# A vision block with routed experts on one core: blocks without a GpSimd drain, fill rows written in the block before, expert stage skewed by two more pairs

## The chip, the cores and the metric

One Trainium2 chip; the program runs on one of its cores, in one launch. The metric is device microseconds of that core for one execution, the median over the runs. The engines are TensorE (PE, with PEld for its weight loads), VectorE (DVE), ScalarE (ACT), GpSimd (POOL) and SyncE (SP), which here only issues transfers. Each engine runs its own instruction stream in order and meets the others through semaphores.

## The reference

The input is 64 images; each is cut into 196 patches of 768 numbers, so there are S = 64 x 196 = 12544 tokens of width D = 256.

```python
h = einsum('bnk,ek->bne', patches, W) + b                  # tokens
h = h + ssm(layernorm(h))                                  # x = A_bar*x + Bu, y = C x + D u
x = layernorm(h)
y1 = ln(x + mha(x)) * g1 + be1                             # 4 heads, attention over the 64 images
# routing: 8 experts, each takes its first S // 8 tokens
gates = softmax(y1 @ wg); idx = argmax(gates)
loc = rank of the token among those of its expert; keep = loc < S // 8
y = (y1 @ w1[idx] + b1[idx]) @ w2[idx] + b2[idx]           # no nonlinearity between
y2 = ln(y1 + where(keep, gate * y, 0)) * g2 + be2
out = h + y2
```

## The kernel before

In the profile a block's end stands at the line at which its scope closes: L155 (weights split, constants built), L304 (after block A), L721 (after block B), L1183 (the program's end).

**Block A** computes the tokens and the state space layer for 49 groups of 256 tokens, and beside it folds each expert's two matrices into one 256 x 256 matrix (`w12`, and `b12` for the biases), since there is no nonlinearity between them.

**Block B** computes attention, the first layer norm, the gate and the token's place in its expert's bin, for 49 groups, with up to six groups in flight. GpSimd writes every group's rows into `bins` in DRAM with two indirect transfers (`send`, L908). A row has 515 numbers: y1, the residual h1, the gate, the token's order S and the token's number (`OFF_I`). At its end GpSimd waits until all have landed (L917 and after), and VectorE makes running counts for the ranks (L1043 to L1051).

**Block C** is the expert stage. It begins with a stretch of set-up: TensorE sums the counts (L1424) and the ranks (L1427 to L1429); VectorE turns the counts into the first free row of each bin (`fi`, L1326) and into two tables that say for each of 106 tiles of 128 rows where its rows are (`tab_r`) and whose weights it takes (`tab_e`, L1345), and then into the threshold beyond which a token is dropped (`tile_thr`, L1360). SP and ACT fill 128 rows behind the last token of each bin (9 transfers, L1231, L1235, L1289), so that a tile may read past a bin's end. TensorE runs 20 matmuls with no use for their result (L1434) as soon as the tables are there.

Then come 53 pairs of tiles. Each engine runs a loop of steps; in step k it does some stages for pair k, others for pair k-1 or k-2 (`k.back(n)`). The stages, with what they wait for:

- SP `load` (L1245): both tiles of a pair into one of 8 row buffers `row`, when the pair 8 earlier has been sent and its transfers have landed (`sent`).
- PE `turn_y` (L1442): 4 transposes of y1 into `c_ps_t`. ACT `y_out` (L1255): their copy into `yt`. PE `experts` (L1454, L1457): 10 matmuls whose weights are picked by registers, loaded from `tab_e` (L1448).
- DVE `keep` (L1366, L1369): gate, or zero for a dropped token. ACT `weighted` (L1263): product times gate.
- DVE `residual` (L1375), `stats` (L1380), `mean` (L1387); ACT `dev` (L1270); DVE `scale` (L1393), `shift` (L1398); ACT `norm` (L1277); DVE `gain` (L1404), `finish` (L1411): layer norm, and the sum with h1 into one of 8 buffers `res`.
- POOL `send` (L1304): two indirect transfers into `out`, with the token numbers read from the row buffer.

The steps of before, from the code of ACT, DVE and PE:

```python
# ACT
for m, stage in ((k, y_out), (k.back(1), weighted), (k.back(2), norm), (k.back(1), dev)):
# DVE
for m, stage in ((k.back(2), shift), (k.back(1), residual), (k.back(1), stats), (k.back(1), mean),
                 (k.back(2), gain), (k, keep), (k.back(2), finish), (k.back(1), scale)):
# PE
for m, stage in ((k.back(1), experts), (k, turn_y)):
```

So PE's order is experts(k-1), turn_y(k), experts(k), and experts(k) needs ACT's copy of what turn_y(k) has just written. An engine's order within a step is fixed; nothing schedules it again. Between steps 8 and 48 the loop is a real one with eight steps in its body.

## Time and profile before

| | |
|---|---|
| median of 3 runs | 1417.65 us (1417.57 to 1417.94) |
| the profiled execution | 1416.46 us |
| its span, first to last instruction | 1414.6 us |
| busy in the span | PE 1261.9, PEld 1142.2, DVE 1030.3, ACT 735.8, POOL 711.5 us |
| mean granted TensorE clock | 0.967 of full |
| block C | from 1152.88 us to the end, 261.7 us |

The profiled execution took 1.19 us less than the median, and 1.86 us of it lie outside the span. Busy times are sums over the whole program, in which four stages with different limits follow each other; the stage that the change touches most is the last, block C, and its set-up.

### The profile page before, as it was taken

The page shows a single profiled execution, that of the slowest core. Times are in us where ns is not written, and L with a number is a line of the kernel's source. Part 1 is how long each engine was busy: PE and PEld are TensorE (multiplying, and loading weights), DVE is VectorE, ACT ScalarE, POOL GpSimd, SP SyncE. Part 2 cuts the span into 40 slices and gives each one's busy share as a digit, 9 for nine tenths or more (in the row PEclk, how much of TensorE's full clock was granted, in tenths as well). Part 3 has the DMA queues.
Part 4 walks back from the last instruction along what each step waited for, and adds up shares of the span by engine and source line. Part 5 has one row for each costly group of instructions (what it writes and reads, how often), then busy time and mean ns, then how long its engine had stood idle before and what let it go on. Part 6 is the DMA issues. An engine that isn't in the chain of part 4 may idle for free. (4 is left out here: it accounts for less than half of the span.)

```text
span 1414.6 us, 37211 instructions
## 1 busy us (share of the span) xinstructions
PE 1261.9 (89%) x11790; PEld 1142.2 (81%) x11791; DVE 1030.3 (73%) x2787; ACT 735.8 (52%) x1515; POOL 711.5 (50%) x913
## 2 busy tenths in 40 slices
PE   2999999999999997699999999999999638788783
PEld 2999999999999997599999999999999525455452
DVE  4578878877887777467777777777777556777774
ACT  3465565555555555354555555455545205665663
POOL 1566656656665663135445544544554323455454
PEclk9999999999999999799999999999999759999997
DMA  7435453545455432122323232322222136666661
GB/s 237 151 113 157 145 188 112 175 138 176 141 157 175 128 104 95 40 72 96 102 92 104 93 100 89 104 97 97 97 97 97 68 109 184 194 182 184 184 185 35
DMA packets 97044, 180.07 MB, mean 127 GB/s; under 512 B 12319, under 2 KB 62497, under 8 KB 95970
## 3 DMA queue, kind: packets, MB, share of 16 engines
q1 hardware_dynamic: 82244, 138.66, 32.6%
q0 software_dynamic: 13312, 39.75, 7.7%
q10 hardware_dynamic: 1440, 1.07, 0.2%
q8 instruction: 23, 0.38, 0.1%
q14 instruction: 25, 0.20, 0.1%
HBM read 112.69 MB, written 67.80 MB: 128 GB/s over the span
## 5 line engine op out<-in xcount | busy, mean ns | idle before, releaser
L476 POOL TENSOR_TENSOR xl<-xf,xh 128x512 fp32r<-128x512 f32 x141 | 178.9, 1298 | 204.6 <-ACT xh L402 204.6
L1304 POOL DMA_INDIRECT out<-res,row x106 | 123.0, 1160 | 116.7 <-DVE res L1411 99.1
L297 PE MATMUL ps_h<-wh,xh 128*128 128x256 f32 x588 | 166.4, 283 | 4.9 <-DVE xl L613 4.9
L297 PE MATMUL ps_h<-wh,xl 128*128 128x256 f32 x588 | 166.4, 283 | 0.0
L297 PE MATMUL ps_h<-wl,xh 128*128 128x256 f32 x588 | 166.1, 283 | 0.0
L1454 PE MATMUL c_ps_y<-w,yt 128*128 x424 | 119.6, 405 | 45.5 <-ACT yt L1255 45.5
L843 ACT ACTIVATE zn<-z,nm_z,rs_z 128x256 f32<-128x256 f32 x98 | 53.6, 594 | 200.6 <-DVE nm_z L972 200.6
L908 POOL DMA_INDIRECT bins<-rows,slot_i x98 | 101.1, 1031 | 60.2 <-POOL slot_i L902 45.2
L1454 PEld LDWEIGHTS c_ps_y<-w,yt 128*128 128x128 f32 x424 | 72.0, 189 | 69.9 <-issue 57.8
L297 PEld LDWEIGHTS ps_h<-wh,xh 128*128 128x128 f32 x588 | 111.9, 190 | 5.6 <-DVE xl L613 5.6
L297 PE MATMUL b<-x2h,wh 128*128 128x256 f32 x392 | 114.3, 292 | 0.0
L297 PEld LDWEIGHTS ps_h<-wl,xh 128*128 128x128 f32 x588 | 111.8, 190 | 0.0
L297 PEld LDWEIGHTS ps_h<-wh,xl 128*128 128x128 f32 x588 | 111.6, 190 | 0.0
L297 PE MATMUL b<-x2l,wh 128*128 128x256 f32 x392 | 110.3, 281 | 0.0
L297 PE MATMUL b<-x2h,wl 128*128 128x256 f32 x392 | 110.3, 281 | 0.0
L926 DVE TENSOR_TENSOR x2l<-ps_o,x2h 128x512 fp32r<-128x512 f32 x49 | 33.9, 691 | 95.2 <-ACT x2h L848 95.2
L882 POOL TENSOR_TENSOR x2b<-x,rows_c 128x512 f32<-128x512 f32 x49 | 63.3, 1292 | 61.2 <-DVE z L958 58.4
L902 POOL CAST slot_i<-small 128x2 int32<-128x2 f32 x49 | 9.0, 184 | 159.5 <-DVE small L1020 159.5
L531 DVE TENSOR_TENSOR_SCAN xs<-decay,xs,bu 128x256 f32<-128x256 f32 x96 | 66.9, 738 | 29.6 <-ACT bu L414 29.4
L438 ACT ACTIVATE nrm_x<-mv_xa,c_eps 128x2 f32<-128x2 f32 x49 | 14.5, 296 | 141.0 <-DVE mv_xa L591 141.0
L492 POOL TENSOR_TENSOR h1b<-h1o,rows_c 128x512 f32<-128x512 f32 x49 | 79.4, 1622 | 10.1 <-DVE h1o L578 10.1
L539 DVE TENSOR_TENSOR sl<-xs,sh 128x512 fp32r<-128x512 f32 x49 | 79.9, 1632 | 0.0
(254 smaller groups left out, 4388.9 us busy)
## 6 DMA issues: line engine op xcount, KB each, us to landing
xf<-xt SPq DMA_DIRECT2D x49, 768.0 KB, 5.3
row<-bins SPq DMA_DIRECT2D x106, 257.5 KB, 3.0
h_dram<-h1b SPq DMA_DIRECT2D x49, 256.0 KB, 5.2
x_dram<-x2o SPq DMA_DIRECT2D x49, 256.0 KB, 5.3
x<-x_dram SPq DMA_DIRECT2D x98, 128.0 KB, 2.8
rows<-h_dram SPq DMA_DIRECT2D x98, 128.0 KB, 2.8
w1s<-w1t SPq DMA_DIRECT2D x8, 1024.0 KB, 6.8
w2s<-w SPq DMA_DIRECT2D x8, 516.0 KB, 5.3
```

The costliest lines, as they stand in the source:

```text
L297: last = nc.tensor.matmul(out_ps, a, b, start=(i == 0), stop=(i == len(terms) - 1))
L438: nc.scalar.activation(nrm_x[:, 0, :], mv_x[:, :, 1], ACT.Sqrt, bias=c_eps[:]).then_inc(x_sd, 1)
L476: last = nc.gpsimd.tensor_tensor(xl[:, p, part], xf[:, p, part], xh[:, p, part].bitcast(F32), ALU.subtract)
L492: nc.gpsimd.tensor_tensor(h1b[:, p], h1o[:, p], r_be2.unsqueeze(1).to_broadcast([P, 2, D]), ALU.add).then_inc(h1b_done, 1)
L531: v.tensor_tensor_scan(xs[:, p, t, :], decay[:, t, bass.ds(m.n() * G % N, G)], bu[:, p, t, :], 0.0 if first else xs[:, 1 - p, t, G - 1:G], ...
L539: v.tensor_tensor(sl[:, p, :], xs[:, p].rearrange("p t g -> p (t g)"), sh[:, p, :].bitcast(F32), ALU.subtract).then_inc(s_lo, 1)
L843: A(zn[:, s, :], z[:, s, :], ACT.Identity, bias=nm_z[:, s:s + 1], scale=rs_z[:, s:s + 1]).then_inc(Q["zn"], 1)
L882: g.tensor_tensor(x2b[:, p], x2[:, p], r_bo.unsqueeze(1).to_broadcast([P, 2, D]), ALU.add).then_inc(Q["x2b"], 1)
L908: g.indirect_dma_start(bins, bass.IndirectOffsetOnAxis(ap=slot_i[:, p, s:s + 1], axis=0), rows[:, p, s, :], None).then_inc(scattered[p], 16)
L926: v.tensor_tensor(xl[:], b_2, xh[:].bitcast(F32), ALU.subtract).then_inc(Q["x2lo"], 1)
L1304: g.indirect_dma_start(out, bass.IndirectOffsetOnAxis(ap=row[:, b, i, OFF_I:OFF_I + 1].bitcast(I32), axis=0), res[:, b, i, :], None, bound ...
L1454: mm(ps_y[p][:, i, :], yt[:, p, i, t * P:(t + 1) * P], w12[:, bass.ds(e, 1), t * D:(t + 1) * D].rearrange("p a d -> p (a d)"), start=(t == ...
```

## The change

It does five things.

2. The fill rows are written at the end of block B, by SP and ACT, and the counts that they need are summed there (PE into `b_4`, DVE into `cnt`, `past`, `fi`, ahead of the running counts for the ranks). GpSimd no longer waits at the end of block B for its transfers; SP does, at the start of block C.
3. In block C, PE runs 40 matmuls without a use in place of 20, and doesn't wait for the tables before them. PE's step becomes turn_y(k), experts(k-1). ACT and DVE take most stages one or two pairs later, in a new order.
4. A row buffer is free for the next load when DVE's `finish` has read it (`res_s`) and GpSimd has copied its two columns of token numbers into `idx` (new stage `index`, L1315 of the changed kernel), not when the transfers out of it have landed.
5. In block A, DVE waits for the experts' second bias (`fb_in`) before its loop, not within the first turn of it.

```diff
-            blk = ...(nc.Block())
+            blk = ...(nc.Block(no_gpsimd_drain=True))      # in all four blocks
@@ block A, DVE
-                        if isinstance(k.t, int):
-                            dve.wait_ge(fb_in, 16)
...
+                dve.wait_ge(fb_in, 16)                      # after the first two x_lo
@@ block B, SP, after its loop
                 run(sp, step, 0, NG + 2, 6, 46)
+                sp.dma_start(bins[BINS:BINS + P, :], fill[:]).then_inc(filled, 16)
+                sp.wait_ge(fi_ready, 1)
+                for e in range(NE // 2):
+                    r = sp.value_load(fi[0:1, e:e + 1], min_val=0, max_val=BINS)
+                    sp.dma_start(bins[bass.ds(r, P), :], fill[:]).then_inc(filled, 16)
@@ block B, ACT, after its loop
+                act.wait_ge(fi_ready, 1)
+                for e in range(NE // 2, NE):
+                    r = act.value_load(fi[0:1, e:e + 1], min_val=0, max_val=BINS)
+                    act.dma_start(bins[bass.ds(r, P), :], fill[:]).then_inc(filled, 16)
@@ block B, GpSimd, after its loop
-                for i in range(2):
-                    pool.wait_ge(scattered[i], 32 * ((NG + 1 - i) // 2))
@@ block B, DVE, after its loop
+                dve.wait_ge(cnt_ps, 1)
+                v.tensor_copy(cnt[:], b_4[:, 0:NE]).then_inc(cnt_out, 1)
+                dve.wait_ge(cnt_out, 1)
+                v.tensor_tensor(past[:], cnt[:], ebase[:], ALU.add).then_inc(past_done, 1)
+                dve.wait_ge(past_done, 1)
+                v.tensor_copy(fi[:], past[:]).then_inc(fi_ready, 1)
@@ block B, PE, after its loop
+                pe.wait_ge(Q["acc"], 2 * NG)
+                pe.wait_ge(Q["k_out"], 2 * NG)
+                mm(b_4[:, 0:NE], ones_b[:], oh_acc[:], start=True, stop=True).then_inc(cnt_ps, 1)
@@ block C, SP
-                (fill rows)
+                for i in range(2):
+                    sp.wait_ge(scattered[i], 32 * ((NG + 1 - i) // 2))
                 sp.wait_ge(filled, 16 * (NE + 1))
                 sp.wait_ge(tab_ready, 1)
...
-                            wait(sp, sent[b], k.turn(DEPTH) * 32)
+                            wait(sp, res_s, k.n() + 1 - DEPTH)
+                            wait(sp, idx_s, k.n() + 1 - DEPTH)
@@ block C, ACT
-                    for m, stage in ((k, y_out), (k.back(1), weighted), (k.back(2), norm), (k.back(1), dev)):
+                    for m, stage in ((k.back(4), dev), (k, y_out), (k.back(4), norm), (k.back(2), weighted)):
@@ block C, GpSimd
+                def index(k):
+                    b = k.slot(DEPTH)
+                    wait(pool, loaded[b], (k.turn(DEPTH) + 1) * 32)
+                    wait(pool, sent[b], k.turn(DEPTH) * 32)
+                    apart(pool, passed["pool"])
+                    g.tensor_copy(idx[:, b, :], row[:, b, :, OFF_I].bitcast(I32)).then_inc(idx_s, 1)
...
+                def step(k):
+                    for m, stage in ((k.back(-1), index), (k, send)):
@@ block C, DVE
-                dve.wait_ge(cnt_ps, 1)                      # counts, past, fi: now in block B
...
-                    for m, stage in ((k.back(2), shift), (k.back(1), residual), (k.back(1), stats), (k.back(1), mean),
-                                     (k.back(2), gain), (k, keep), (k.back(2), finish), (k.back(1), scale)):
+                    for m, stage in ((k.back(3), residual), (k.back(2), keep), (k.back(3), stats), (k.back(4), gain),
+                                     (k.back(3), mean), (k.back(4), finish), (k.back(3), scale), (k.back(3), shift)):
@@ block C, PE
-                pe.wait_ge(tab_ready, 1)
-                for _ in range(20):
+                for _ in range(40):
                     mm(ps_c[:], wh[:, 0:P], wh[:, 0:2 * D], start=True, stop=True)
...
-                    for m, stage in ((k.back(1), experts), (k, turn_y)):
+                    for m, stage in ((k, turn_y), (k.back(1), experts)):
```

The loops of ACT, DVE and PE run to `PAIRS + 4`, `PAIRS + 4` and `PAIRS + 1`. Buffers `rows`, `slot_i`, `cnt` and `fi` move to a scope that outlives block B.

On TensorE, around the end of the first pair's expert matmuls in block C (`c_ps_y0` is the product of an even pair, `c_ps_t0` and `c_ps_t1` hold the transposes of even and odd pairs). Before:

```order
L1454 MATMUL c_ps_y0<-w12,yt 128x256
L1457 ISA
L1457 MATMUL c_ps_y0<-b12s,two_rows 128x256
L1442 MATMUL c_ps_t1<-ident,row 128x128 x4
L1448 TENSOR_LOAD tab_e
```

And now, at the same place:

```order
L1471 MATMUL c_ps_y0<-w12,yt 128x256
L1474 ISA
L1474 MATMUL c_ps_y0<-b12s,two_rows 128x256
L1459 MATMUL c_ps_t0<-ident,row 128x128 x4
L1465 TENSOR_LOAD tab_e
```

Behind the product of pair 0 stood the transposes of pair 1; now those of pair 2 stand there, and pair 1's were done ahead of it.

On VectorE, one step of block C before:

```order
L1398 SCALAR_TENSOR_TENSOR c_nm<-c_mv,c_rs 128x2
L1375 TENSOR_TENSOR c_z<-c_py,row 128x512
L1380 BN_STATS c_st<-c_z 128x6 x2
L1387 BN_AGGR c_mv<-c_st 128x2 x2
L1404 TENSOR_TENSOR c_zg<-c_zn,rows_c 128x512
L1366 TENSOR_TENSOR c_below<-row,tile_thr 128x2
L1369 TENSOR_TENSOR gk<-c_below,row 128x2
L1411 TENSOR_TENSOR res<-c_zg,row 128x512
L1393 RECIPROCAL c_rs<-c_ve 128x2
```

And now:

```order
L1394 TENSOR_TENSOR c_z<-c_py,row 128x512
L1385 TENSOR_TENSOR c_below<-row,tile_thr 128x2
L1388 TENSOR_TENSOR gk<-c_below,row 128x2
L1399 BN_STATS c_st<-c_z 128x6 x2
L1423 TENSOR_TENSOR c_zg<-c_zn,rows_c 128x512
L1406 BN_AGGR c_mv<-c_st 128x2 x2
L1430 TENSOR_TENSOR res<-c_zg,row 128x512
L1412 RECIPROCAL c_rs<-c_ve 128x2
L1417 SCALAR_TENSOR_TENSOR c_nm<-c_mv,c_rs 128x2
```

The nine operations are the same. Between an operation and the one that needs it there now stands another, except for the two pairs of very small ones.

On SyncE, where block B ends and block C begins (L721 is the block's end). Before:

```order
L786 DMA rows<-h_dram 64x2x256 x10
L721 UNCONDITIONAL_BRANCH
L1228 UNCONDITIONAL_BRANCH
L1231 DMA bins<-fill 128x515
L1234 TENSOR_LOAD fi
```

And now:

```order
L789 DMA rows<-h_dram 64x2x256 x10
L801 DMA bins<-fill 128x515
L804 TENSOR_LOAD fi
L804 ISA x2
L805 ISA
```

The fill transfers stand ahead of the block's end now.

## Rows read from the trace of the kernel before

**Rows 1.** The page's chain that ended last, by engine, line and share of the span.

```profile
PE c_ps_y L1454 8%; PE c_ps_y L1457 2%; PE c_ps_t L1442 2%; ACT yt L1255 2%; POOL out L1304 0%; DMA bins<-fill 0%; DMA row<-bins 0%; ACTq L1288 0%; ACT c_py L1263 0%; DVE c_st L1380 0%; ACTq L1289 0%; DVE c_z L1375 0%; SPq L1242 0%; DVE res L1411 0%; DVE c_zg L1404 0%
```

**Rows 2.** Windows: us, busy PE, PEld, DVE, ACT, POOL, clock, DMA share, GB/s.

```profile
1144.00:1164.00 20.00, 5.55 (x15) 3.50 (x16) 9.99 (x24) 0.00 (x0) 0.22 (x1) 0.50 0.33 119
1168.00:1390.00 222.00, 177.08 (x732) 111.69 (x732) 170.10 (x559) 133.42 (x307) 113.34 (x98) 1.00 0.62 179
```

**Rows 3.** Timeline, one pair in the loop: start, us, operation, idle before.

```profile
1279.21 0.60 ACT L1255 ACTIVATE yt<-c_ps_t 128x512 f32<-128x512 f32 x1 [0.66 <-PE c_ps_t L1442]
1280.03 1.13 PE L1454 MATMUL c_ps_y<-w,yt 128*128 x4 [0.86 <-ACT yt L1255]
...
1282.78 0.66 PE L1442 MATMUL c_ps_t<-ident,row 128*128 128x128 f32 x4
```

**Rows 4.** Timeline of DVE, one step in the loop.

```profile
1278.12 0.66 DVE L1404 TENSOR_TENSOR c_zg<-c_zn,rows_c 128x512 f32<-128x512 f32 x1
1278.70 0.16 DVE L1366 TENSOR_TENSOR c_below<-row,tile_thr 128x2 f32<-128x2 f32 x1
1278.97 0.69 DVE L1411 TENSOR_TENSOR res<-c_zg,row 128x512 f32<-128x512 f32 x1
1279.58 0.16 DVE L1393 RECIPROCAL c_rs<-c_ve 128x2 f32<-128x2 f32 x1
1279.78 0.16 DVE L1398 SCALAR_TENSOR_TENSOR c_nm<-c_mv,c_rs 128x2 f32<-128x2 f32 x1
1280.57 0.70 DVE L1375 TENSOR_TENSOR c_z<-c_py,row 128x512 f32<-128x512 f32 x1 [0.63 <-ACT c_py L1263]
1281.30 0.75 DVE L1380 BATCH_NORM_STATS2 c_st<-c_z 128x6 f32<-128x256 f32 x2
1282.23 0.25 DVE L1387 BATCH_NORM_AGGREGATE c_mv<-c_st 128x2 f32<-128x6 f32 x2 [0.18 <-DVE c_st L1380]
```

**Rows 5.** Timeline of POOL, two sends in the loop.

```profile
1278.15 1.49 POOL L1304 DMA_INDIRECT out<-res,row  x1 [0.30 <-issue]
1280.54 0.97 POOL L1304 DMA_INDIRECT out<-res,row  x1 [0.91 <-DVE res L1411]
```

**Rows 6.** GpSimd's DRAINs, by line: min/median/max ns, first and last start.

```profile
L155 POOLq DRAIN  x1: 12399/12399/12399, 11.0 to 11.0; - x1
...
L289 POOLq DRAIN  x1: 96/96/96, 25.0 to 25.0; - x1
...
L721 POOLq DRAIN  x1: 8074/8074/8074, 1144.6 to 1144.6; - x1
...
L1183 POOLq DRAIN  x1: 8720/8720/8720, 1405.7 to 1405.7; - x1
```

**Rows 7.** Timeline, the end of block B and the start of C.

```profile
1136.93 0.47 POOL L890 TENSOR_TENSOR oh_acc<-oh_acc,oh 128x8 bf16<-128x8 bf16 x2 [1.16 <-PE ps_r L1145]
...
1153.53 0.17 DVE L1326 CAST fi<-nt 128x8 int32<-128x8 f32 x1
...
1154.88 4.55 ACTq L1289 DMA_DIRECT2D bins<-fill  x4
...
1160.32 0.22 DVE L1345 TENSOR_SCALAR tab_e<-tile_e 128x106 int32<-128x106 f32 x1
...
1160.60 7.03 PE L1434 MATMUL ps_c<-wh 128*128 128x512 f32 x20 [5.52 <-DVE tab_e L1345]
...
1163.70 8.00 SPq L1245 DMA_DIRECT2D row<-bins  x8
...
1167.90 0.66 PE L1442 MATMUL c_ps_t<-ident,row 128*128 128x128 f32 x4 [0.27 <-DMA row<-bins]
...
1169.54 1.13 PE L1454 MATMUL c_ps_y<-w,yt 128*128 x4 [0.99 <-ACT yt L1255]
```

**Rows 8.** Timeline, the last pair.

```profile
1390.56 1.13 PE L1454 MATMUL c_ps_y<-w,yt 128*128 x4 [0.78 <-ACT yt L1255]
...
1400.24 0.72 DVE L1411 TENSOR_TENSOR res<-c_zg,row 128x512 f32<-128x512 f32 x1
```

More of the change, by code:

```diff
@@ L180, in build @@
             a_arg = pre_sem("decay_arg")
-            blk = pre.enter_context(nc.Block())
+            blk = pre.enter_context(nc.Block(no_gpsimd_drain=True))
             @blk.sync
@@ L347, in build @@
             HALF = FK // 2 * D
-            blk = pa.enter_context(nc.Block())
+            blk = pa.enter_context(nc.Block(no_gpsimd_drain=True))
             h1_grp, x2_grp = (t.rearrange("(g s p) d -> g p s d", s=2, p=P) for t in (h1_dram, x2_dram))
@@ L718, in build @@
         patches.close()
+        rows = sb("rows", [P, 2, 2, ROW])
+        slot_i = sb("slot_i", [P, 2, 2], I32)
+        cnt, past = sb("cnt", [P, NE]), sb("past", [P, NE])
+        fi = sb("fi", [P, NE], I32)
+        scattered = [sem(f"b_scattered{i}") for i in range(2)]
+        cnt_ps, cnt_out, past_done, fi_ready, filled = (
+            sem("c_" + s) for s in ("count_ps", "count", "past", "fill_rows", "filled"))
         with ExitStack() as pb_:
@@ L739, in build @@
             y1t = sb("y1t", [P, FT * G], F32, pb_)
-            rows = sb("rows", [P, 2, 2, ROW], F32, pb_)
             mx = sb("mx", [P, 2 * H], F32, pb_)
@@ L761, in build @@
             r_loaded = [sem(f"b_row_loaded{i}") for i in range(2)]
-            scattered = [sem(f"b_scattered{i}") for i in range(2)]
             names = ("x2b x2T x2hi x2lo v_ps v_out q_ps q_out k_ps k_out s_ps max sub exp et_ps "
@@ L1280, in step @@
                 def step(k):
-                    for m, stage in ((k, y_out), (k.back(1), weighted), (k.back(2), norm), (k.back(1), dev)):
+                    for m, stage in ((k.back(4), dev), (k, y_out), (k.back(4), norm), (k.back(2), weighted)):
                         if m.valid(PAIRS):
                             stage(m)
-                act.wait_ge(fi_ready, 1)
-                for e in range(NE // 2, NE):
-                    r = act.value_load(fi[0:1, e:e + 1], min_val=0, max_val=BINS)
-                    act.dma_start(bins[bass.ds(r, P), :], fill[:]).then_inc(filled, 16)
-                run(act, step, 0, PAIRS + 2, *PAIR_LOOP, DEPTH)
+                run(act, step, 0, PAIRS + 4, *PAIR_LOOP, DEPTH)
             @blk.gpsimd
@@ L1303, in send @@
                     for i in range(2):
-                        g.indirect_dma_start(out, bass.IndirectOffsetOnAxis(
-                                                 ap=row[:, b, i, OFF_I:OFF_I + 1].bitcast(I32), axis=0),
+                        g.indirect_dma_start(out, bass.IndirectOffsetOnAxis(ap=idx[:, b, i:i + 1], axis=0),
                                              res[:, b, i, :], None, bounds_check=S - 1, oob_is_err=False).then_inc(sent[b], 16)
-                run(pool, send, 0, PAIRS, *PAIR_LOOP, DEPTH)
+                def step(k):
+                    for m, stage in ((k.back(-1), index), (k, send)):
+                        if m.valid(PAIRS):
+                            stage(m)
+                run(pool, step, -1, PAIRS, *PAIR_LOOP, DEPTH)
                 for i in range(DEPTH):
@@ L1423, in _ @@
                 mm = nc.tensor.matmul
-                mm(ps_c[:, 0:NE], ones_b[:], oh_acc[:], start=True, stop=True).then_inc(cnt_ps, 1)
                 for i in range(2):
```

29 lines of the change are left out of this document (10 added, 19 removed).

## The prediction

> **What bounds the kernel now.** I read the chain that ended last first. Its largest engine shares lie in block C, the expert stage: the matmuls with the expert weights, the transposes and ACT's copy `yt` take turns on it [rows 1]. Then the windows: over the 222 us of the pairs TensorE is busy 177 us, VectorE 170 us, ScalarE 133 us, GpSimd 113 us, the transfer engines 0.62, and the clock is granted in full (the 2.4 GHz level) [rows 2]. No engine is full, so a handover sets the pace. The timeline of one pair shows it: TensorE is through with the transposes, ACT copies (1279.21, 0.60 us), and only then, 0.86 us idle later, the matmuls of the same pair start [rows 3]. From the first matmul of pair 0 (1169.54 [rows 7]) to that of pair 52 (1390.56 [rows 8]) it is 221.0 us, 4.25 us a pair.
>
> The second place is the two ends of block C. GpSimd's DRAIN at the end of block B takes 8.07 us from 1144.6, that at the program's end 8.72 us from 1405.7 [rows 6], and in both all other engines stand. In the set-up behind the first, the loads begin at 1163.70, 3.2 us after the tables (1160.54), because the last fill transfer was issued at 1159.43 [rows 7].
>
> **The pace of a pair.** With transposes one pair ahead, TensorE needs no copy of what it has just written. Its own work is 1280.03 to 1282.78, 2.75 us, for ten matmuls, and at most 0.66 us for the transposes, which overlap the next matmuls by an unknown part [rows 3]: 3.2 (estimate) to 3.4 us. The register loads for the weights run on its queue meanwhile, as now.
>
> VectorE does the same nine operations. In the new order an operation mostly doesn't follow the one that it needs. Rows 4 show what that saves: `c_below` starts 0.08 us before `c_zg` ends, but `c_mv` waits 0.18 us for `c_st`, and `c_z` waits 0.63 us for ACT. I add up: `c_z` 0.62, `c_below` and `gk` 0.27, `c_st` 0.67, `c_zg` 0.58, `c_mv` 0.17, `res` 0.61, `c_rs` 0.20, `c_nm` 0.08 (durations less 0.08 us of overlap, or distances of starts) [rows 4]. That is 3.20 us.
>
> ScalarE has 133.42 / 53, about 2.5 us [rows 2]. Its loop with VectorE: from `shift`, `norm` takes 1.1 us and may end 1.35 us later, while VectorE does `residual`, `keep` and `stats`, 1.6 us; then `gain` needs it. So 0.25 us is left there. `dev` takes 0.3 us behind `mean`, under `finish` (0.61 us). Both are covered, narrowly; without cover each would cost its excess in every pair.
>
> GpSimd's pair: two sends of 0.97 us with 0.30 us ahead of the second [rows 5], as much ahead of the next operation, and the new copy of two columns, at most 0.2 us (the small copies of block B, and `gk`, are of that size): 2.74 us. With sends of 1.49 us it is 3.78 us. What makes a send long is in the rows: the one at 1278.15 began 0.03 us after VectorE's `c_zg`, which ends at 1278.78, and took 1.49 us; the one at 1280.54 began 0.03 us before `c_z` and took 0.97 us, though `c_z` ran beside it [rows 4, 5]. A send that starts under such an operation waits for its end. The GPSIMD Engine Reference of the Trainium skill (section 1, Specifications) says that GpSimd shares its SBUF interfaces with VectorE and contends with VectorE instructions that have two SBUF inputs. By that rule, the trace agrees: `c_z`, `c_zg` and `res` have two.
>
> The three operations fill 2.05 us of a 3.3 us pair, against 4.25 us now. But `send` starts 0.9 us after `res` ends [rows 5], which is behind the next `c_z`; its second half meets the end of `c_zg` and waits some 0.2 us. I count 3.1 us for GpSimd, just below the others.
>
> Transfers: 0.62 x 4.25 = 2.6 us of engine share a pair, so 0.80 at 3.3 us. Loads are freed at `finish`, four steps of VectorE before TensorE's step for that buffer, some 8.6 us ahead; they need about 5 us (4.2 us from the first issue to the transposes now [rows 7]). Hidden.
>
> I take 3.3 us a pair, between VectorE's 3.2 and TensorE's 3.4. **Gain: 52 x (4.25 - 3.3) = 49.4 us.**
>
> **The tail.** In the new order the last pair goes through more steps behind its matmuls. By my schedule these start 2.3 us after `shift` of step 51; then four steps of 3.2 us, and `norm`, `gain`, `finish` 2.7 us: `res` ends 13.2 us after the matmuls' start. Now it is 1400.96 - 1390.56 = 10.4 us [rows 8]. **Cost 2.8 us.** Bounds: 0 and 6.
>
> **The change of blocks B to C.** The last count is added at 1137.40 [rows 7]; one small matmul and three small VectorE operations put `fi` at 1138.3. From `fi`'s end (1153.70) to the end of ACT's last fill issue (1159.43) it is 5.7 us now [rows 7], so ACT reaches the block's end at 1144.0; VectorE, 0.6 us later than now with its running counts, and GpSimd are done by 1142.8. A barrier without a DRAIN: 0.4 us. Block C starts at 1144.5 in place of 1152.9. From `fi` to the tables it is 6.84 us [rows 7]: tables at 1151.3. The fills have landed by then (1144.0 and at most 4.3 us, the distance from 1159.43 to 1163.70 [rows 7]); the loads start about 0.8 us behind the tables, 1152.1. Now the matmuls of pair 0 also need pair 1's transposes, so two more loads, 1.1 us apart (8.00 us for 8 [rows 7]): 1152.1 + 4.2 + 2.2 + 0.45 = 1158.95 instead of 1169.54. **Gain 10.6 us.** The 40 idle matmuls start near 1146.1; 20 took 7.03 us from the low clock [rows 7], 40 take about 11.3 us, to 1157.4: ready in time, and the clock is up. Had they not been made free of the tables, they would end at 1162.6 and cost 4 us.
>
> **The program's end.** The DRAIN of 8.72 us goes, GpSimd's wait for its last transfers stays. **Gain 8.7 us.**
>
> **The program's start.** DRAIN at L155 ran from 11.0 to 23.4, under the constants (VectorE ends at 24.5), so its removal gains nothing. But L289's DRAIN, 0.10 us now [rows 6], becomes the first one after eight GpSimd transfers. What does a DRAIN cost? 98 transfers since the last: 8.07 us; 106: 8.72 us [rows 6]. The difference, 0.65 / 8, is 0.081 us for each, and 98 x 0.081 = 7.9. So it goes by the number of transfers, and eight cost 0.65 us. **Cost 0.7 us.** Bounds: 0, and 7.4 us if the cost were fixed. L155's end fits the first: it came 7.3 us after GpSimd's last transfer was generated at 16.1, but within 1 us after the last of them landed.
>
> Block A to B: SyncE comes last there, GpSimd's DRAIN is covered. The moved `fb_in` wait: VectorE comes to it at 30.5 and its next work is at 33.2; 0, at most 1.
>
> **Sum.** -49.4 + 2.8 - 10.6 - 8.7 + 0.7 = -65.2 us. The profiled execution took 1416.46, so 1351.3; the median of the runs is 1.2 higher than it: **1352.4 us.**
>
> **The rivals.**
> *GpSimd becomes the bound.* Sends fall under VectorE's operations twice a pair and take 1.49 us: 3.78 us a pair. For: in a shorter pair these operations leave fewer gaps. Against: sends are tied to `res` and so keep their place in the step. Time: 1352.4 + 52 x 0.48 = 1377. Chance 0.17.
> *The DRAIN's work comes back.* A fixed price at L289, +6.7 us, 1359; or the 204 transfers are taken back within the sends, 0.08 us each: 0.16 us a pair and, if it came in one lump of 8.7 us, the eight `res` buffers (26 us) would cover it. Chance 0.12 for 1357 to 1362.
> *The pace doesn't change*, because the loop of `shift`, `norm`, `gain` or ACT's `weighted` two steps late puts in a wait as long as the removed one: 1401.8. Against: the slack above. Chance 0.04, with what lies between.
> *Slower: the clock.* It falls to the 1.2 GHz level when the idle matmuls end (1157.4) and TensorE waits for loads, and stays there. It stood at 0.50 in the set-up of C and at 1.00 through the pairs with TensorE 80% busy [rows 2]. At half clock a pair takes 6.6 us, +3.3 us each; 20 such pairs of 53 eat the gain; all give 1524. Against: TensorE will be busier than in those rows. Chance 0.02.
> My forecast, 3.2 to 3.5 us a pair, 1346 to 1364: 0.65.
>
> **Numbers.** The range runs from 3.2 us a pair with a shorter tail (1344) to the first rival (1378): what is left out is some 0.15, mostly above. This kernel's runs differ by 0.03%, and 0.2% (2.8 us) tells a change; all cases but the last are faster by more: faster 0.97, within 0.2% 0.01, slower 0.02.
>
> **What would show it.** Starts of pair 0's and pair 52's expert matmuls 172 us apart; VectorE with no idle time before `c_z` and `c_mv`, over 90% busy; the first load at 1152; no GpSimd DRAIN at the ends of B and C; L289's at 0.75 us; sends of 0.97 us first and up to 1.3 us second. I'd be wrong if VectorE waited for `c_zn`, if loads were late at the transposes, or if GpSimd's sends had no idle time before them.

## The result and the profile after

The changed kernel takes 1357.12 us (median of 4 runs, 1356.27 to 1357.88) against 1417.61 us (1417.35 to 1417.94). The ratio is 0.9573, 95% interval 0.9556 to 0.9590: 60.5 us less. The profiled execution took 1356.27 us and its span is 1354.4 us, so the spans differ by 60.2 us.

The chain that ended last, in the page of the changed kernel, has moved from TensorE and ScalarE to VectorE [rows 1]:

```profile
DVE c_st L1399 2%; DVE res L1430 2%; DVE c_below L1385 1%; DVE c_mv L1406 1%; DVE gk L1388 1%; DVE c_z L1394 1%; DVE c_zg L1423 0%; ACT c_zn L1292 0%; DVE c_rs L1412 0%; PE c_ps_y L1471 0%; DVEq L81 0%; DMA row<-bins 0%; DVE c_nm L1417 0%; POOL out L1323 0%; PE c_ps_t L1459 0%
```

Two windows of the changed kernel, the set-up and the pairs (columns as in [rows 2]). Over the pairs TensorE is busy 166.6 of 172 us, where it was 177 of 222; the clock in the set-up has a mean of 0.80 in place of 0.50:

```profile
1144.00:1164.00 20.00, 15.04 (x59) 11.21 (x59) 13.17 (x30) 1.19 (x2) 0.99 (x4) 0.80 0.67 193
1164.00:1336.00 172.00, 166.55 (x718) 108.91 (x719) 156.72 (x543) 131.53 (x300) 117.56 (x142) 1.00 0.75 221
```

The timeline of one pair on TensorE and ScalarE, which answers to [rows 3]. TensorE does the transposes and goes on with the matmuls of the pair before (1253.57); ScalarE's copy runs under them, and no idle time stands ahead of the next matmuls:

```profile
1253.07 0.66 PE L1459 MATMUL c_ps_t<-ident,row 128*128 128x128 f32 x4
...
1253.57 1.03 PE L1471 MATMUL c_ps_y<-w,yt 128*128 x4
...
1253.77 0.60 ACT L1270 ACTIVATE yt<-c_ps_t 128x512 f32<-128x512 f32 x1 [0.24 <-issue]
...
1256.21 0.66 PE L1459 MATMUL c_ps_t<-ident,row 128*128 128x128 f32 x4
```

VectorE and GpSimd in the same step (answers to [rows 4, 5]). VectorE's operations stand back to back, without an idle entry. GpSimd's first send takes 0.98 us; the second began 0.32 us after the start of `c_zg` and took 1.20 us:

```profile
1254.05 0.69 DVE L1394 TENSOR_TENSOR c_z<-c_py,row 128x512 f32<-128x512 f32 x1
...
1254.64 0.98 POOL L1323 DMA_INDIRECT out<-res,c_idx  x1 [0.55 <-issue]
1254.66 0.17 DVE L1385 TENSOR_TENSOR c_below<-row,tile_thr 128x2 f32<-128x2 f32 x1
...
1254.94 0.75 DVE L1399 BATCH_NORM_STATS2 c_st<-c_z 128x6 f32<-128x256 f32 x2
...
1255.60 0.68 DVE L1423 TENSOR_TENSOR c_zg<-c_zn,rows_c 128x512 f32<-128x512 f32 x1
...
1255.92 1.20 POOL L1323 DMA_INDIRECT out<-res,c_idx  x1 [0.30 <-issue]
1256.19 0.24 DVE L1406 BATCH_NORM_AGGREGATE c_mv<-c_st 128x2 f32<-128x6 f32 x2
1256.35 0.66 DVE L1430 TENSOR_TENSOR res<-c_zg,row 128x512 f32<-128x512 f32 x1
```

The end of block B and the start of C (answers to [rows 7]). The fills (ACTq L875) now stand ahead of the tables (`tab_e`), and the first load follows the tables by 0.8 us. The transposes at 1161.16 are those of pair 1; pair 0's stand at 1159.39, right behind the last of the 40 idle matmuls (the ones with no use):

```profile
1138.88 0.47 POOL L902 TENSOR_TENSOR oh_acc<-oh_acc,oh 128x8 bf16<-128x8 bf16 x2 [1.15 <-PE ps_r L1160]
...
1140.03 0.17 DVE L1056 CAST fi<-past 128x8 int32<-128x8 f32 x1
...
1141.16 5.09 ACTq L875 DMA_DIRECT2D bins<-fill  x4
...
1148.42 11.12 PE L1451 MATMUL ps_c<-wh 128*128 128x512 f32 x40
...
1153.55 0.22 DVE L1364 TENSOR_SCALAR tab_e<-tile_e 128x106 int32<-128x106 f32 x1
...
1154.60 14.91 SPq L1260 DMA_DIRECT2D row<-bins  x14
...
1161.16 0.66 PE L1459 MATMUL c_ps_t<-ident,row 128*128 128x128 f32 x4 [1.18 <-DMA row<-bins]
...
1162.83 1.12 PE L1471 MATMUL c_ps_y<-w,yt 128*128 x4 [1.01 <-ACT yt L1270]
```

The last pair (answers to [rows 8]), and GpSimd's DRAIN at L289 (answers to [rows 6]; at the ends of the blocks it has none):

```profile
1336.83 1.12 PE L1471 MATMUL c_ps_y<-w,yt 128*128 x4
...
1348.76 0.72 DVE L1430 TENSOR_TENSOR res<-c_zg,row 128x512 f32<-128x512 f32 x1
```

```profile
L289 POOLq DRAIN  x1: 83/83/83, 24.7 to 24.7; - x1
```

The two traces, by the terms of the prediction's sum:

| stretch | before | after | difference | predicted |
|---|---|---|---|---|
| to the last count (`oh_acc`) | 1137.40 | 1139.35 | +1.95 | +0.7 |
| last count to pair 0's matmuls | 32.14 | 23.48 | -8.66 | -10.6 |
| pair 0's matmuls to pair 52's | 221.02 | 174.00 | -47.0 | -49.4 |
| those to the end of `res` | 10.40 | 12.65 | +2.25 | +2.8 |
| end of `res` to the end of the span | 13.6 | 4.9 | -8.7 | -8.7 |
| sum | | | -60.2 | -65.2 |

A pair takes 3.35 us. Most are 3.13 or 3.23 us from the next, but 18 of the 52 distances are over 3.4 us, up to 4.36.

One thing in the trace has no counterpart before. SyncE's queue, which issues the row loads, is held again and again in the expert stage: 53 of its instructions there take 0.6 to 0.73 us, 38 of them 0.70 or more, and they are of any kind. The rows of its instructions by line (ns min/median/max) show it at a register MOVE, which took 29 ns every time before:

```profile
L1260 SPq MOVE row<-bins x106: 3/29/723, 1154.5 to 1328.6; - x106
```

### The profile page after: what moved, and what is told of

Its sections match the earlier page's. It is cut to its first block and busy times, and to the rows that moved or that the text cites. A ratio compares the mean times of both kernels' runs of the same rounds, so it can differ in the third digit from the quotient of the medians.

```text
span 1354.4 us, 37450 instructions
## 1 busy us (share of the span) xinstructions
PE 1261.2 (93%) x11810; PEld 1147.7 (85%) x11811; DVE 1020.7 (75%) x2787; ACT 737.2 (54%) x1515; POOL 718.3 (53%) x966
## 5 line engine op out<-in xcount | busy, mean ns | idle before, releaser
L1323 POOL DMA_INDIRECT out<-res,c_idx x106 | 116.5, 1099 | 61.6 <-issue 46.2
L1471 PEld LDWEIGHTS c_ps_y<-w,yt 128*128 128x128 f32 x424 | 71.9, 189 | 24.4 <-issue 12.0
```

What stands on the lines that cost most here:

```text
L1323: g.indirect_dma_start(out, bass.IndirectOffsetOnAxis(ap=idx[:, b, i:i + 1], axis=0), res[:, b, i, :], None, bounds_check=S - 1, oob_is_er ...
L1471: mm(ps_y[p][:, i, :], yt[:, p, i, t * P:(t + 1) * P], w12[:, bass.ds(e, 1), t * D:(t + 1) * D].rearrange("p a d -> p (a d)"), start=(t == ...
```

## The experiments

Theory A: the slow pairs come from late rows. Around them the transposes start 5.2 to 5.7 us after SyncE issued the pair's first load, in the 3.13 us pairs of the start over 8 us after. SyncE's holds make the loads late, and TensorE's reads of the expert numbers, queued behind the transposes, add 1.7 us to a late row. Rival B: VectorE, disturbed by GpSimd, sets the pace. The ratios are against the kernel before, run in the same group (medians 1417.32 us for the first four of these runs, 1417.40 for the next four, 1417.00 for the last four).

| run | median us | ratio, 95% | us a pair | holds |
|---|---|---|---|---|
| the changed kernel | 1357.12 | 0.9556 to 0.9590 | 3.35 | 53 |
| `sent_back` | 1385.96 | 0.9761 to 0.9819 | 3.91 | 16 |
| `no_sends` (one run) | 1347.22 | | 3.26 | 0 |
| `regs_first` | 1351.39 | 0.9521 to 0.9553 | 3.25 | 33 |
| `depth10` | 1352.29 | 0.9524 to 0.9556 | 3.38 | 39 |
| `nodrain_only` | 1400.56 | 0.9868 to 0.9903 | 4.25 | 2 |
| `skew_only` | 1403.68 | 0.9887 to 0.9936 | 3.91 | 6 |
| `regs_unroll` | 1345.36 | 0.9480 to 0.9514 | 3.13 | 0 |
| `skew_less` | 1351.40 | 0.9521 to 0.9555 | 3.26 | 2 |
| `drain_end` (one run) | 1359.93 | | 3.24 | 0 |
| `fills_late` | 1357.60 | 0.9548 to 0.9590 | 3.32 | 0 |
| `warm20` (one run) | 1356.60 | | 3.30 | 1 |
| `combined` | 1343.94 | 0.9459 to 0.9496 | 3.13 | 0 |

"us a pair" is the distance of pair 0's and pair 52's expert matmuls over 52 and "holds" the number of SyncE's instructions between them that take 0.6 to 0.75 us, both in the profiled execution. By this count the kernel before has 1. Two issues of a transfer lie above it, 0.88 us in `no_sends` and 1.13 us in `regs_first`. The column mixes two things. In the changed kernel, `sent_back`, `regs_first` and `depth10` the holds stand on all kinds of instructions, register work that otherwise takes 0.02 to 0.1 us among them. The few in the kernel before, `nodrain_only`, `skew_only`, `skew_less` and `warm20` are reads of the table `tab_r`, which take 0.27 us otherwise, and two issues of a transfer.

### Buffers given back when the transfers have landed (`sent_back`)

```diff
-                            wait(sp, res_s, k.n() + 1 - DEPTH)
-                            wait(sp, idx_s, k.n() + 1 - DEPTH)
+                            wait(sp, sent[b], k.turn(DEPTH) * 32)
```

> The changed kernel, but a row buffer goes back to the loads when its transfers out have landed, as before the change. Theory A (the loads are the late ones in the slow pairs: 5.2 to 5.7 us from the issue to the transposes there): rows are asked for some 5 us later in every turn of eight buffers, so the mean distance of the pairs rises from 3.35 us to 3.6 us or more, and the time to 1370 us or more. Rival B (the slow pairs come from VectorE and GpSimd disturbing each other, the loads have slack): 3.35 us a pair as now, 1357 us.

1385.96 us, 28.8 us slower than the changed kernel. Theory A holds, and the size is more than lateness alone. The timeline of TensorE shows the first late row, of pair 8: 1.5 us of idle time, and then the four matmuls that took 1.03 to 1.13 us take 2.07. The windows show what came with it: the granted clock is 1.00 up to there and 0.55 over the next 10 us, the 1.2 GHz level for most of them:

```profile
1180.37 1.13 PE L1470 MATMUL c_ps_y<-w,yt 128*128 x4
...
1183.32 1.11 PE L1458 MATMUL c_ps_t<-ident,row 128*128 128x128 f32 x4 [1.52 <-DMA row<-bins]
1185.30 2.07 PE L1470 MATMUL c_ps_y<-w,yt 128*128 x4 [0.86 <-ACT yt L1269]
```

```profile
1180.00:1182.00 2.00, 1.81 (x7) 1.04 (x6) 1.97 (x9) 1.66 (x5) 1.54 (x3) 1.00 0.80 226
1182.00:1192.00 10.00, 7.82 (x20) 5.22 (x21) 5.56 (x19) 3.28 (x8) 5.22 (x8) 0.55 0.63 181
```

The distances from pair 5's matmuls on are 3.14, 6.20, 5.93, 4.10, 3.14 us: this row, 1.5 us late, costs 6.8 us. The Trainium skill (TensorE: Matmul & The Clock Gate, section Part 1: The HAM clock gate) tells of a clock that goes down to 1.2 GHz when TensorE idles; here the rows put a price on it. But not each late row does this. The clock is at the lower level three times between the pairs, for 10.2, 6.8 and 3.4 us, while TensorE waits 0.4 us or more ahead of an instruction 26 times; and ahead of pair 1's transposes and pair 0's matmuls it waits 1.40 and 0.98 us and the clock stays at 1.00. Most of the 28.8 us are then the waits themselves, by these rows.

### GpSimd's transfers left out (`no_sends`)

```diff
-                        g.indirect_dma_start(out, bass.IndirectOffsetOnAxis(ap=idx[:, b, i:i + 1], axis=0),
-                                             res[:, b, i, :], None, bounds_check=S - 1, oob_is_err=False).then_inc(sent[b], 16)
+                        g.tensor_copy(idx2[:, b, i:i + 1], idx[:, b, i:i + 1]).then_inc(sent[b], 16)
```

> The changed kernel, but GpSimd's indirect transfers are left out: two small copies of a column stand in for them, and out isn't written by them. SyncE's queue shows 53 holds of 0.72 us in the expert stage, on any kind of instruction, where the kernel before has none. Theory A1: GpSimd's transfers cause them (79% of that time lies within sends): without sends no holds, loads early, pairs 3.13 to 3.2 us apart, 1348 us. Rival A2: the holds come from SyncE's own loads standing back to back: they stay, and the distance stays above 3.25 us.

1347.22 us and no hold: A1, as far as this run goes. But the pairs don't reach 3.13 us. Without any hold they settle at 3.25, with 3.65 once in eight; and later runs with the transfers in them have no such holds either (below). So the transfers are not enough to cause them. That 79% of the holds' time lies within sends says little: sends fill 67% of that stretch. The pace answers rival B, though: without GpSimd's transfers it is 3.26 us, and with them but without holds 3.24 (`drain_end`, below), so GpSimd doesn't slow VectorE's step.

### Expert numbers read ahead of the transposes (`regs_first`)

```diff
-                    for m, stage in ((k, turn_y), (k.back(1), experts)):
+                    for m, stage in ((k.back(1), regs), (k, turn_y), (k.back(1), experts)):
```

(`regs` holds the two `value_load`s of `experts`, nothing else is moved.)

> The changed kernel, but TensorE reads the expert numbers of pair k-1 ahead of the transposes of pair k, not behind them. In the slow pairs the reads (1.7 us on the queue) begin when the rows of the next pair arrive, so a late row costs twice. Theory A: slow pairs get up to 1.1 us shorter and the mean falls from 3.35 to 3.2 us, 1350 us. Rival: the reads are hidden by the matmuls at hand and VectorE or the loads alone set the pace: 1357 us.

1351.39 us, 5.7 us less, with 33 holds still there. The distances are 3.13 at first, then 3.21 to 3.24 and 3.6 once in eight: the late rows no longer show. At the start of block C it gains too: pair 0's matmuls follow pair 1's transposes by 0.49 us, against 1.67 us (1161.16 to 1162.83) in the changed kernel. The profile puts that wait down to ACT's copy, but the copy that these matmuls need, pair 0's, had ended at 1160.62; it is the two reads that end at 1162.66. Timeline of `regs_first`:

```profile
1159.34 0.66 PE L1459 MATMUL c_ps_t<-ident,row 128*128 128x128 f32 x4 [1.30 <-DMA row<-bins]
1159.83 1.03 PE L1475 MATMUL c_ps_y<-w,yt 128*128 x4
```

### Ten buffers (`depth10`)

```diff
-DEPTH = 8
+DEPTH = 10
```

> The changed kernel with ten buffers of rows and of results in place of eight. Theory A as a matter of latency: rows are asked for two pairs (6.5 us) earlier, they are never late, 3.13 to 3.24 us a pair, 1349 us. Rival A3: SyncE's issue (2.2 us a pair and the holds of 0.72 us) is itself the bound in the slow stretches: more buffers only move it, the mean stays above 3.3 us, 1356 us.

1352.29 us: the rows' lateness is one of latency, and more buffers cure it, against A3. Three of the four runs are 1352.1 to 1352.4; the profiled one is 1358.13. In it ScalarE does nothing from 1191.2 to 1195.2, where its loop begins, TensorE idles 3.13 us for it, and over the next 10 us the clock has a mean of 0.59. What stopped ScalarE isn't shown. Apart from this the distances are 3.13, then 3.24, with 3.5 to 3.65 once in ten, which is once in a turn of the loop.

### Only the DRAINs removed (`nodrain_only`)

```diff
-            blk = ...(nc.Block())
+            blk = ...(nc.Block(no_gpsimd_drain=True))      # the kernel before, in all four blocks
```

> The kernel before with no_gpsimd_drain in all four blocks and nothing else. By the two exposed DRAINs (8.07 and 8.72 us) it gains 16.8 us: 1400.5 us. If the DRAIN's work came back in the sends or at the next DRAIN, it gains 8 us less or more; L289's DRAIN stays at 0.08 to 0.10 us as in the changed kernel. Rival: SyncE's holds of 0.72 us come from the missing DRAINs; then they stand here too, in the expert stage at 4.25 us a pair.

1400.56 us, the sum of the two exposed DRAINs to within 0.1 us. L289's DRAIN takes 83 ns here too. Two holds, both on table reads, and none on other instructions: the missing DRAINs alone don't cause them.

### Only the orders of the expert stage (`skew_only`)

The three `for m, stage in (...)` lines of ACT, DVE and PE from the change, in the kernel before; the loops of ACT and DVE run to `PAIRS + 4`.

> The kernel before with the three new orders of TensorE, ScalarE and VectorE in the expert stage alone; row buffers go back when their transfers have landed. Without late rows the pairs would be 3.3 us apart, gain 47 us less 2.3 us of tail, 1373 us. By the run in which only the give-back was undone (3.91 us a pair) rows are late: gain 17.5 us less 2.3 us, 1402 us; with the DRAINs kept no more. A gain of over 40 us would say that the late give-back hurts only together with the copy of the token numbers.

1403.68 us (runs from 1401 to 1412): the second of the two cases. The pace is 3.91 us, as in `sent_back`, with the same distances of 5 to 6 us, and three falls of the clock. So the new order takes 0.34 us off each pair where, with early buffers, it takes 0.90.

### The expert stage written out (`regs_unroll`)

```diff
 def run(eng, step, first, last, lo, hi, u=2):
+    if u == DEPTH:
+        for c in range(first, last):
+            step(At(0, c, u))
+        return
```

> The run with the expert numbers read ahead of the transposes, and the expert stage written out for all 53 pairs, without the loop of eight steps. In the loop a pair takes 3.24 us against 3.13 us outside it, and every eighth 3.6 us. Theory: VectorE's addresses and waits worked out from the loop's register, and the branch, cost these 0.11 and 0.4 us: 3.14 us a pair and 5.7 us less, 1345.7 us. Rival: the 3.24 us come from rows being loaded beside (outside the loop at the end no loads run): the same 1351.4 us; or fetching so many instructions holds engines up: slower.

1345.36 us. All distances but the last are 3.13 or 3.14 us: the theory of the loop holds, both the 0.11 us in every pair and the 0.4 us once in eight were the loop's. The run writes out the loops of all engines. That VectorE's is the one that counted is read from traces with the loop and without holds: in `drain_end` VectorE stands idle 0.44 us before `c_z` once in eight pairs, on nothing but its own issue, and `no_sends`, where GpSimd has little to do, is no faster a pair. Written out, TensorE is the bound; the window of its pairs has it busy all the time:

```profile
1162.00:1322.00 160.00, 160.00 (x716) 107.72 (x715) 150.68 (x542) 130.49 (x300) 125.21 (x140) 1.00 0.80 239
```

No hold stands in it. GpSimd's timeline shows how close the first rival came: a copy that waits behind the last send, then 1.39, 0.30, 0.97 us, in all 3.13 us. The first send now starts under `res` and waits for its end:

```profile
1252.50 0.97 POOL L1327 DMA_INDIRECT out<-res,c_idx  x1 [0.30 <-issue]
1253.47 0.31 POOL L1319 COPY c_idx<-row 128x2 int32<-128x2 int32 x1
1253.94 1.39 POOL L1327 DMA_INDIRECT out<-res,c_idx  x1 [0.16 <-POOL c_idx L1319]
1255.63 0.98 POOL L1327 DMA_INDIRECT out<-res,c_idx  x1 [0.30 <-issue]
```

It is also why from the end of `res` to the end of the span it is 6.8 us in this run and 4.9 us in the changed kernel: GpSimd is one send behind. This isn't the writing out. `regs_first`, `skew_less`, `fills_late` and `warm20`, with the loop, have the same 6.8 us, `drain_end` has it ahead of its DRAIN, and in all of them 43 of the 53 first sends take over 1.3 us, in the changed kernel 5. Where few rows are late GpSimd is at the edge; in the changed kernel the late rows give it time to catch up.

### ScalarE and VectorE one pair earlier (`skew_less`)

```diff
-                    for m, stage in ((k.back(4), dev), (k, y_out), (k.back(4), norm), (k.back(2), weighted)):
+                    for m, stage in ((k.back(3), dev), (k, y_out), (k.back(3), norm), (k.back(1), weighted)):
```

(and every stage of DVE one `back` less, both loops to `PAIRS + 3`.)

> The changed kernel with ScalarE's weighted, norm, dev and all of VectorE's stages one pair earlier. Buffers are then given back one pair (3.2 us) earlier against the matmuls, too. The tail gets 3.1 us shorter; with rows asked for 3.2 us earlier fewer of them are late, up to 2 to 5 us more: 1350 to 1354 us. Rival: ScalarE, which then takes its copy for the next transposes behind the product of the pair at hand, holds TensorE up: over 3.4 us a pair, 1360 us.

1351.40 us, in the range expected, but by luck. From pair 52's matmuls to the end of `res` it is 11.73 us against 12.65, 0.9 us less and not 3.1. The rest is the pace, 3.26 us, and that isn't shown to come from the edit: the changed kernel's own code, in an execution without holds, has 3.24 us a pair and about 1351.0 us (`drain_end`, next). This run has no holds of the changed kernel's kind either. Against that it gains nothing.

### The DRAIN at the program's end put back (`drain_end`)

```diff
-            blk = pc.enter_context(nc.Block(no_gpsimd_drain=True))
+            blk = pc.enter_context(nc.Block())                     # block C only
```

> The changed kernel with GpSimd's DRAIN at the program's end alone put back. No DRAIN stands between it and the start, so 204 transfers lie ahead of it, not 106. If its price goes by all transfers since the last DRAIN (0.081 us each), it takes 16.5 us, 1373.5 us. If the transfers of block B have been cleared up otherwise (the one pause of 1.6 us within a send of the expert stage), it takes 8.7 us or less, 1366 us.

The DRAIN takes 8.89 us with 204 transfers since the start, nearly the 8.72 us of 106. So my price for each transfer since the last DRAIN is wrong, unless the pause of 1.6 us had dealt with block B's transfers.

```profile
L1201 POOLq DRAIN  x1: 8887/8887/8887, 1348.9 to 1348.9; - x1
```

The time is 1359.93 us. Less the DRAIN it is 1351.0, 6.1 us under the changed kernel, and SyncE's instructions are the same as there. In this execution they aren't held:

```profile
L1260 SPq MOVE row<-bins x106: 29/29/29, 1152.8 to 1318.9; - x106
```

Its distances are 3.13, then 3.22, with 3.65 once in eight, mean 3.24. So the pace without holds is 3.24 us with just the order and the buffers of the change. From pair 8 on the loads are issued 8.1 to 8.7 us ahead of the transposes, the 8.6 us of the prediction.

### The fills moved back (`fills_late`)

The two pieces of block B that issue `bins<-fill` (SP, ACT) stand at the start of block C again; `fi` stays in block B.

> The changed kernel with the nine fill transfers moved back to the start of the expert stage; the counts stay in block B. The block then ends when VectorE is through with its running counts, 1.5 us earlier. SyncE and ScalarE issue the fills there in 5 to 6.5 us, and they land 3.5 us later (before: 1154.88 to 1163.70), 10.2 us behind the stage's start, while the tables need 7.0 us: the first load comes 3.2 us later against the start, so 1.7 us later in all: 1358.8 us. By my prediction's sum the early fills are worth 2.4 to 3.2 us. Rival: no difference, since ScalarE's issue only moves across the barrier.

1357.60 us. The block ends 1.8 us earlier against the last count, the first load comes 3.9 us behind the tables, and pair 0's matmuls start 24.4 us after the last count against 23.5: 1.0 us lost where I had expected 1.7. But the next two distances are 5.93 and 4.59 us, not 3.23 and 3.13: the 40 idle matmuls end at 1157.8, 2.9 us before the first transposes, and the clock falls to 0.50. This costs 4.2 us. By these rows the early fills, with the 40 idle matmuls set for them, are worth 5.2 us; the medians can't say it, since the changed kernel has 53 holds and this one none.

### Twenty idle matmuls (`warm20`)

```diff
-                for _ in range(40):
+                for _ in range(20):
```

> The changed kernel with 20 idle matmuls in place of 40. They end at 1155.5 in place of 1159.5, and TensorE idles until the first rows are there (1159). If the granted clock falls in that time, the first pairs run at half speed for some microseconds: 1358 to 1361 us, and much more only if it never rises. If it doesn't fall, 1356.9 us, within what executions of this kernel differ by.

1356.60 us, with the same 5.93 us behind pair 0: the clock falls. The windows before, in and after that time (the figure behind POOL's count is the granted clock):

```profile
1157.00:1159.00 2.00, 0.00 (x0) 0.00 (x0) 1.30 (x4) 0.00 (x0) 0.40 (x1) 1.00 0.73 207
1159.00:1167.00 8.00, 5.77 (x16) 3.74 (x17) 2.58 (x5) 1.19 (x2) 0.37 (x2) 0.55 0.83 245
1167.00:1169.00 2.00, 2.00 (x7) 1.12 (x6) 0.00 (x0) 0.00 (x0) 0.00 (x0) 0.50 0.70 224
...
1171.00:1173.00 2.00, 2.00 (x11) 1.49 (x11) 1.81 (x7) 0.00 (x0) 0.00 (x0) 1.00 0.83 227
```

It costs 2.7 + 0.3 us in the first two distances. The whole is 5.6 us above `drain_end` without its DRAIN; 2.6 us of it lie ahead of the last count, in blocks A and B, which are the same in both kernels. As a comparison of medians this pair says little; the clock rows say it.

### Together (`combined`)

The edits of `regs_first`, `regs_unroll` and `skew_less`.

> Three edits of the runs so far together: expert numbers read ahead of the transposes, the stage written out without its loop, ScalarE's and VectorE's stages one pair earlier. The pair stays at TensorE's 3.13 us; the tail gets 3.1 us shorter: 1342.3 us. Rival: GpSimd, at 3.13 us a pair in the run written out (1.39 + 0.30 + 0.97 + 0.31 + 0.16), is the bound now and lags, so the shorter tail is eaten by its last sends: 1345 us.

1343.94 us, 13.2 us (1.0%) below the changed kernel and 5.2% below the kernel before, the best of all. Some 6 us of the 13.2 are the changed kernel's holds and not these edits: against its 1351.0 us without them it is 7.1 us. The pace is 3.13 us. The tail is 11.8 us, 0.9 us shorter, not 3.1, and 6.8 us follow for GpSimd's last sends: the rival's result, though its reason is only half of it.

## Why the prediction was right, and where its terms were off

**The main steps held.** The handover between transposes, copy and matmuls was the pace; with it gone, the pairs stand 3.35 us apart (predicted 3.3, between VectorE's and TensorE's sums). One of the prediction's own signs of being wrong did come, loads late at the transposes. The exposed DRAINs were worth their rows, 8.07 and 8.72 us, and nothing of it came back that is seen in the time. The rule for sends held: the one that starts under `c_zg` ends 0.84 us behind its end (0.86 before) and takes 1.20 us, where I wrote that it "waits some 0.2 us". The tail cost 2.25 us (predicted 2.8). Of the early start of C, the loads follow the tables by 0.8 us as predicted.

**The pace, a gain 2.4 us smaller than its term.** I called the loads hidden, with 8.6 us ahead and 5 needed. That margin was real at the start and then used up: in the slow pairs the transposes start 5.2 to 5.7 us after the issue. What goes with it are the holds in SyncE's queue, which the trace before doesn't have. Without them (`drain_end`) the margin stays above 8 us and it is 52 x 3.24 = 168.6 us in place of 174.0, which is 3.0 us below my 171.6. TensorE's floor, for which I had added up 3.2 to 3.4 us, is 3.13 us, and VectorE's (3.20) no more than that, when no loop registers and no branch stand in the way (`regs_unroll`).

**The register reads, left out.** I wrote that they "run on its queue meanwhile, as now". In the new order they stand behind transposes that wait for a row, so they don't. From pair 1's transposes to pair 0's matmuls I had 0.45 us; it is 1.67, and 0.49 in `regs_first`. This 1.2 us is the largest part of what B to C is short (1.9 us). The rest: 0.2 us more from the first load to pair 1's transposes (6.56 against 6.4), 0.2 us for the barrier and the fills, 0.3 us for the tables. The idle matmuls cost nothing in the end. I called them "ready in time" at 1157.4, though by my own sum the first rows were due at 1156.3; in the trace pair 0's transposes follow the last of them without a wait, about 0.5 us late, but pair 1's, which pair 0's matmuls need as well, still wait 1.18 us for their rows. In the pairs `regs_first` takes 169.0 us against 174.0, though part of that may be its fewer holds; `drain_end`, with the reads where they were, takes 168.6. So the reads cost something only where a row is late or, at the start, awaited.

**L289, the wrong model of a DRAIN.** Predicted 0.7 us, measured none (83 ns, with eight transfers before it). "It goes by the number of transfers" fitted two rows (98 and 106) and failed on both tests: 8 cost nothing (but these are plain transfers, not indirect ones), 204 cost 8.89 us. The one trace of uncleared transfers that I see is a pause of 1.6 us between the two sends of the eighth pair (GpSimd's idle time 1.92 for 0.30 us). It stands in every kernel here that sends and has no DRAIN at the end of block B (1.7 us for 1.9 in `regs_unroll` and `combined`), and in neither that has it:

```profile
1202.44 1.30 POOL L1323 DMA_INDIRECT out<-res,c_idx  x1 [1.92 <-issue]
```

It was covered. What a DRAIN's 8 us are made of stays open.

**Blocks A and B, +1.95 us where only L289 was expected.** Two things stand in it. The first count starts 0.35 us later (617.9 against 617.6 us); over all the runs it lies between 616.1 and 618.8, also where the code is the same, so this part says nothing. From there on the distance grows evenly through block B, by some 0.03 us a group, and this is the change: from the first count to the 85th of 98 it is 455.3 to 455.6 us in the changed kernel and all ten runs with its block B, and 454.1 to 454.3 us in the kernel before, `nodrain_only` and `skew_only`, which have the old one. It isn't the missing DRAINs (`nodrain_only`) and not the fill transfers (`fills_late` has it too). The prediction had no term for it, 1.6 us by the block's end. What of the change does it wasn't tested; that some buffers moved to another scope is one candidate. The counts of the changed kernel, then of `nodrain_only` (the two times are the starts of the first and the last one, 521.2 and 519.6 us apart):

```profile
L902 POOL TENSOR_TENSOR oh_acc<-oh_acc,oh x98: 189/199/202, 617.9 to 1139.1; 128x8 bf16<-128x8 bf16 x98
```

```profile
L890 POOL TENSOR_TENSOR oh_acc<-oh_acc,oh x98: 187/197/201, 617.0 to 1136.6; 128x8 bf16<-128x8 bf16 x98
```

**The end of the program, right by luck.** 8.7 us were predicted and measured. But the DRAIN is only one part of the stretch, and GpSimd's lag the other: it is 4.9 us behind `res` in the changed kernel, as forecast, because late rows let GpSimd catch up, and 6.8 us in the runs without them.

**What the number owes to luck.** `drain_end` without its DRAIN, 1351.0 us, is the changed kernel's code without holds, 1.4 us from my 1352.4. By its stretches the errors cancel: the pairs gain 3.0 us more than I had, the tail costs 0.3 us less, blocks A and B are 0.5 us better, but B to C is 1.7 us short and the end 1.9 us. The holds, which nobody foresaw, then add some 6 us.

**Which part brought what.** The DRAINs alone 16.8 us, the orders alone 13.7 us, and the early give-back 28.8 us on top of all the others: without it the orders are starved of rows, and a few of the late rows also take the clock down. My sum laid the whole 49.4 us to the order and dealt with the give-back in one sentence on the loads. The number was right, the share wasn't told. The three add up to 59.3 of 60.5 us, but not because each stands alone: the early fills, by rows 5.2 us, are in none of them, and the holds take some 6 us back.

**The rivals.** GpSimd as the bound at 3.78 us a pair (0.17) didn't come about, but without late rows its two sends (1.39 and 0.97 us), their gaps and the copy (0.31 us, where I had at most 0.2) already take 3.13 us, level with TensorE when the stage is written out. The clock (0.02) does fall to the 1.2 GHz level, as the runs with late rows, late fills and 20 idle matmuls show; but it comes back while the matmuls go on, so where the rows tell it costs 3 to 7 us a time (the wait included) and not 3.3 us in each pair.

**What stays open.** What holds SyncE's queue. Holds on all kinds of instructions stand in the changed kernel, `sent_back`, `regs_first` and `depth10`. The last three ran on one chip, together with `no_sends`, which has none; which chip the changed kernel's own trace is from isn't on record. The other eight runs were on two other chips, and none has them, though `drain_end`, `warm20` and `fills_late` have both the transfers and the loop. So on the one chip the holds need GpSimd's transfers, as far as one run says it; whether they also go with the chip, or with the program as it was loaded, no run tells apart. The same doubt lies on comparisons across the groups: the changed kernel has no runs beside `drain_end`, `skew_less` or `combined`. All its four runs lie 5 to 7 us above 1351 us, about what the holds explain; its time without holds rests on one run of `drain_end`. Open too are what a DRAIN's 8 us are made of and what slows block B.

## What to carry to other kernels

When a stage is skewed to take a handover off the path, count how early its inputs are asked for in the new, shorter period: here the order alone gave 13.7 us and the earlier return of the buffers 28.8 us more. A late row costs more than its lateness: one of 1.5 us cost 6.8 us, since the clock fell as well. Anything that an engine reads through its own queue (register loads) belongs ahead of the instruction that waits for data, not behind it. And once the pace is set by an engine that is always busy, the loop's own register work (0.11 us a pair) and its branch (0.4 us) are the next term. Before crediting an edit with a gain, look in both traces whether the base was disturbed: `regs_first`, `depth10` and `skew_less` are 5 to 6 us faster than the changed kernel, and none of them is faster than its 1351.0 us without holds.

## What the runs showed of the hardware

- In `sent_back` a wait of 1.52 us on TensorE, with one of 0.86 us behind it, went with a fall of the granted clock from 1.00 to 0.50 for 10.2 us; four matmuls that took 1.13 us took 2.07. Waits of 1.40 and 0.98 us at the start of the same stage left it at 1.00. With TensorE idle for 2.9 and 4.0 us ahead of the first rows (`fills_late`, `warm20`) it fell both times.
- GpSimd's DRAIN cost 8.07, 8.72 and 8.89 us after 98, 106 and 204 indirect transfers, and 0.083 us after eight plain transfers and 9 us of idle time.
- SyncE's queue can be held 0.6 to 0.73 us at a time, on instructions of 0.03 us too, up to 53 times in 174 us, in one program and not in another with the same SyncE code, which ran at another time and perhaps on another chip.
- GpSimd's indirect send takes 0.97 us, but one that starts under a VectorE operation with two inputs ends 0.84 to 0.86 us behind that operation's end: 1.20, 1.39 or 1.49 us in all.
- In a loop with eight steps in its body a step took 3.22 to 3.24 us against 3.13 us written out, and the first step of a turn 0.4 us more; two register reads on TensorE's queue took 1.5 us (1161.17 to 1162.66 in the changed kernel).
